# Flamingo block (gated cross-attention and gated feed-forward): scores, transposes and attention products of a query tile issued in one run each, turned probabilities kept in place

## What is computed

```python
# x: (16, 512, 512), context: (16, 120, 512)
Q, K, V = heads(layernorm(x) @ W_q.T), heads(ctx @ W_k.T), heads(ctx @ W_v.T)
scores = Q @ K^T / sqrt(32) - slope[head] * (query_pos - key_pos)       # 512 x 120 for each head
e = exp(scores - max(scores))
attn = e / (1.0 + sum(e))
x = x + tanh(g_xattn) * ((attn @ V) @ W_o.T)
n = layernorm(x);  prev = n shifted by one token
r = sigmoid((mu_r*n + (1-mu_r)*prev) @ W_r.T)
k = relu((mu_k*n + (1-mu_k)*prev) @ W_k.T) ** 2
x = x + tanh(g_ffn) * r * (k @ W_v.T)
```

## Time and profile before

| | |
|---|---|
| Time, median of 3 runs | 1523.38 us (1522.04 to 1524.48) |
| Span of the profiled execution, first to last instruction | 1519.6 us |
| TensorE matmul busy | 1442.7 us (95%) |
| TensorE weight loads busy | 1083.1 us (71%) |
| VectorE busy | 1161.5 us (76%) |
| ScalarE busy | 889.5 us (59%) |
| GpSimd busy | 721.3 us (47%) |

### The profile page before, as it was taken

The page is one execution under the profiler, slowest core; times in us unless marked ns, Lnnn a source line. Parts: engine busy times, 40 slices in busy tenths (PEclk is TensorE's granted clock), DMA queues, the critical chain, the costliest instruction groups (busy, mean ns, idle before and its releaser), DMA issues.

```text
span 1519.6 us, 32873 instructions
## 1 busy us (share of the span) xinstructions
PE 1442.7 (95%) x10864; PEld 1083.1 (71%) x10864; DVE 1161.5 (76%) x2889; ACT 889.5 (59%) x2928; POOL 721.3 (47%) x766
## 2 busy tenths in 40 slices
PE   7988899999999999999999999999999999999998
PEld 6876767677676767667686766767676676768667
DVE  4456868787887868798786879878687887868775
ACT  5147474665747465574747566473756657475662
POOL 0003455545455555545555464545546454555542
PEclk9999999999999999999999999999999999999999
DMA  8721001020200102020010202011020101001000
GB/s 270 215 66 49 8 29 50 0 76 0 56 20 28 49 0 76 0 56 20 28 49 14 62 0 56 20 36 41 14 62 0 56 20 53 23 27 50 1 30 28
DMA packets 53009, 65.95 MB, mean 43 GB/s; under 512 B 23024, under 2 KB 29168, under 8 KB 52976
## 3 DMA queue, kind: packets, MB, share of 16 engines
q1 hardware_dynamic: 52976, 65.52, 14.6%
HBM read 40.87 MB, written 24.64 MB: 43 GB/s over the span
## 4 chain that ended last, share of the span: by engine, by line
PE 48%; DVE 34%; issue 11%; ACT 3%; DMA 2%; DVEq 1%; SPq 0%; POOL 0%; ACTq 0%; POOLq 0%
PE rotating L401 33%; DVE probs L1038 7%; PE probs_bank L561 5%; DVE diff L1100 4%; PE score_bank L460 4%; DVE mix_k L1095 4%; PE attn_bank L575 3%; DVE relu L1100 3%; DVE square L1095 2%; PE score_bank L401 2%; ACT probs L773 2%; DVE mask_in L1137 2%; DVE stats L1008 2%; DVE norm L1017 2%; DVE xs L1064 2%
## 5 line engine op out<-in xcount | busy, mean ns | idle before, releaser
L773 ACT ACTIVATE probs<-probs,neg_max 128x120 f32<-128x120 f32 x1024 | 391.2, 385 | 29.6 <-DVE neg_max L1042 29.6
L1320 POOL TENSOR_TENSOR probs<-probs,recip 128x960 f32<-128x960 f32 x128 | 229.7, 1794 | 237.5 <-DVE recip L1053 237.5
L401 PE MATMUL rotating<-mixed_key,w_key 128*128 128x512 f32 x720 | 205.0, 413 | 24.8 <-ACT gated L825 24.8
L401 PE MATMUL rotating<-w_proj,attn_t 128*128 128x512 f32 x768 | 220.9, 417 | 2.9 <-DVE xnt_or_act L1023 2.0
L781 ACT COPY probs_t<-probs_bank 120x512 f32<-120x512 f32 x256 | 149.8, 585 | 121.3 <-PE probs_bank L561 121.1
L1038 DVE SCALAR_TENSOR_TENSOR probs<-mask_in,score_bank 128x120 f32<-128x120 f32 x1024 | 213.0, 269 | 9.5 <-PE score_bank L460 9.5
L401 PE MATMUL rotating<-w_value,xnt_or_act 128*128 128x512 f32 x720 | 202.3, 409 | 10.2 <-DVE xs L1064 10.2
L401 PE MATMUL rotating<-w_gate,mixed_gate 128*128 128x512 f32 x768 | 209.7, 409 | 0.0
L401 PE MATMUL rotating<-xnt_or_act,w_query 128*128 128x256 f32 x1536 | 198.7, 286 | 0.5 <-DVE xnt_or_act L1023 0.5
L773 ACT ACTIVATION_READ_ACCUMULATOR probs<-probs,neg_max 128x1 f32 x1024 | 194.0, 189 | 0.0
L401 PEld LDWEIGHTS rotating<-xnt_or_act,w_query 128*128 128x128 f32 x1536 | 187.7, 191 | 1.9 <-DVE xnt_or_act L1023 0.8
(11 more groups left out here) (126 smaller groups left out, 2167.7 us busy)
## 6 DMA issues: line engine op xcount, KB each, us to landing
xs<-in_x_dram SPq DMA_DIRECT2D x64, 256.0 KB, 2.9
out_dram<-gated SPq DMA_DIRECT2D x64, 256.0 KB, 3.0
value_scratch<-gated SPq DMA_DIRECT2D x16, 240.0 KB, 2.6
mask_in<-in_mask_dram SPq DMA_DIRECT2D x16, 240.0 KB, 2.6
keys_t<-key_scratch SPq DMA_DIRECT2D x16, 240.0 KB, 3.6
values<-value_scratch SPq DMA_DIRECT2D x16, 240.0 KB, 3.8
probs<-in_ctx_t_dram SPq DMA_DIRECT2D x6, 480.0 KB, 7.0
key_scratch<-query_t SPq DMA_DIRECT2D x12, 240.0 KB, 5.1
```

Source lines behind the costliest of these rows:

```text
L401: mm = pe.matmul(bank, stationary(a, c), moving(b, c), start=(i == 0), stop=(i == MATMULS - 1))
L773: e = act.activation(probs[:, t % 2, head, :], probs[:, t % 2, head, :], ACT.Exp, bias=neg_max[:, t % 2, head:head + 1], accum_out=sums[:, ...
L1320: pool.tensor_tensor(part, part, recip[:, t % 2, heads].unsqueeze(2).to_broadcast((P, H // 2, NK)), ALU.mult)\
```

## The change

The changed kernel computes the same thing with the same instructions on every engine; what changes is their order on TensorE, one buffer, and one wait on VectorE.

- `with_scores` becomes `all_scores`: all 16 products of a tile stand together, and the use that they were woven into follows whole.
- In `with_attention` the portions become 3, 3, 3, 3 (from 4, 3, 3, 2), and the four `attend` groups follow behind the last portion, where before `attend(g - 1)` stood behind `turn_probs(g)` and its portion.
- The scores of tile 2 stand right behind the attention of tile 0 and ahead of `key` 3; before they stood behind it.
- `probs_t` is no longer a buffer of its own with two slots by g. It lies over `probs` in one buffer `probs_room`, with a slot for each tile parity and each group. The transposed group is written over heads that have been transposed already; `probs` starts 128 elements later to make that safe.
- Since a slot of `probs` now holds what `attend` reads, `bias(b, t, 0)` waits for the attention of tile t - 2 (`attn_done`), where before it waited for that tile's transposes and exponentials.

```diff
-        probs = sb("probs", [P, 2, H, NK])
-        probs_t = sb("probs_t", [NK, 2, J, P])
+        HEAD_ROOM = G * J * (P - NK)
+        probs_room = sb("probs_room", [P, 2, HEAD_ROOM + H * NK])
+        probs = probs_room[:, :, HEAD_ROOM:].rearrange("p a (h k) -> p a h k", h=H)
+        probs_t = probs_room[0:NK].rearrange("k a (g j q) -> k a g j q", g=G, j=J)
...
-                                   values[:, head * HD:(head + 1) * HD], probs_t[:, g % 2, j, :],
+                                   values[:, head * HD:(head + 1) * HD], probs_t[:, t % 2, g, j, :],
...
-                def with_scores(t, what, tile, portions):
-                    at = 0
+                def all_scores(t):
                     for g in range(G):
                         scores(b, t, g)
-                        use(what, tile, range(at, at + portions[g]))
-                        at += portions[g]
-
-                def with_attention(t, what, tile, portions=(4, 3, 3, 2)):
+                def with_attention(t, what, tile, portions=(3, 3, 3, 3)):
                     at = 0
                     for g in range(G):
                         turn_probs(b, t, g)
                         use(what, tile, range(at, at + portions[g]))
                         at += portions[g]
-                        if g > 0:
-                            attend(b, t, g - 1)
-                    attend(b, t, G - 1)
-
-                with_scores(0, "gate", 0, (3, 3, 3, 3))
+                    for g in range(G):
+                        attend(b, t, g)
+                all_scores(0)
+                use("gate", 0)
                 use("gate", 1)
                 use("key", 0)
-                with_scores(1, "key", 1, (3, 3, 3, 3))
+                all_scores(1)
+                use("key", 1)
                 with_attention(0, "key", 2)
+                all_scores(2)
                 use("key", 3)
-                with_scores(2, "proj", 0, (3, 3, 3, 3))
+                use("proj", 0)
                 use("value", 0)
                 with_attention(1, "value", 1)
-                with_scores(3, "gate", 2, (4, 4, 4, 0))
+                all_scores(3)
+                use("gate", 2)
...
-                act.copy(probs_t[:, g % 2], probs_bank[0:NK, :].rearrange("k (j q) -> k j q", j=J))\
+                act.copy(probs_t[:, t % 2, g], probs_bank[0:NK, :].rearrange("k (j q) -> k j q", j=J))\
...
-                        dve.wait_ge(probs_turned, (b * QT + t - 1) * G)
-                        dve.wait_ge(exp_done, (b * QT + t - 1) * G)
+                        dve.wait_ge(attn_done, b * QT + t - 1)
```

More of the change, by code:

```diff
@@ L138, in flamingo_block @@
         wv_split = mixed_gate
-        ctx_raw = probs[:].rearrange("p a h k -> p (a h k)").rearrange("p (a c k) -> p a c k", a=4, k=CK)
+        ctx_raw = probs_room[:].rearrange("p a n -> p (a n)")[:, 0:2 * CT * CK]\
+            .rearrange("p (a c k) -> p a c k", a=2, k=CK)
         ctx_split = [xnt_or_act[:].rearrange("p s c t -> p (s c t)")[:, i * 2 * CT * CK:(i + 1) * 2 * CT * CK]
```

## The result

| | before | after |
|---|---|---|
| Time, median | 1523.38 us (1522.04 to 1526.69, 11 runs) | 1526.84 us (1525.75 to 1529.84, 11 runs) |
| Span of the profiled execution | 1519.6 us | 1523.9 us |

The account below looks back on a forecast made before the run. Bound: TensorE between 715.88 and 744.54 of a loop batch, VectorE before and ScalarE then VectorE after. 0.54 + 0.08 = 0.62 us a batch; 15 x 0.6 = 9, less 2 for batch 0: 1523.4 + 7 = 1530 us, range 1517 to 1536.

Parts of the forecast that it names:

- TensorE's savings become waits outside the middle stretch: Loop batch: TensorE savings, 4.0 us in TensorE time alone, can count only between 715.88 and 744.54, where TensorE shows no wait.
- Score run of 1.10 us: Scores of one tile in one run hold TensorE for 1.10 us, 1.3 to 1.4 us less TensorE time a tile.
- Attention run of 1.19 us: Four attention groups in a run hold TensorE for 1.19 us, a further group costing 0.28.
- Fourth transposes at the same place, held by ScalarE's list: Tile 0: fourth transposes start at 725.66 as before, waiting for a copy behind `act_split(1)`; about 1.3 us saved becomes waiting.
- Attention later, since it has been moved behind them: Tile 0: attention ends at 728.13 instead of 727.34, 0.8 us later, two attention groups having moved behind the fourth transposes.
- The chain `key` 3, relu 3, square 3, low part 3 delays `value` 0: After tile 0's attention, through ScalarE and GpSimd: `value` 0 starts at about 736.06, 0.54 us later than before.
- Nobody collects the early scores of tile 2: VectorE's list has tile 1's reciprocals ahead of tile 2's bias, so tile 2's scores ahead of `key` 3 go uncollected.
- The new wait on `attn_done` costs nothing: VectorE's bias: zero cost, as tile t - 2's attention already precedes tile t's scores on TensorE; without that cover, up to 1.19 us.
- Batch 0 gives 2 us: First batch, without relu chain or `act_split`: savings can count there, taken as 2 us of gain, between 0 and 4.0.
- The terms cancel: 1520.5 to 1526.5: No-change rival for the whole kernel: shift within -0.1 and +0.3 us a batch, 1520.5 to 1526.5 us, chance 0.25.
- Outside the middle stretch a saving just becomes a longer wait: Loop batch before 715.88 and after 744.54: a TensorE saving there only lengthens a wait and does not count.
- a sign of being wrong: Counted from tile 1's scores: prediction wrong if `value` 0 starts before +19.6, transposes' waits don't appear, or VectorE's chain changes length.

Follow-up runs that it names:

- e6: Changed kernel with the copy of tile 0's third group of transposed probabilities ahead of act_split(1) in ScalarE's list; 1516.52 us, ratio 0.9958.
- e3: Changed kernel with the attention groups woven between the transposes again (portions 4, 3, 3, 2); 1521.53 us, ratio 0.9984.
- e5: Changed kernel with only its attention part kept, scores woven as before the change and tile 2's behind key 3; 1532.63 us, ratio 1.0060.
- e1: Changed kernel with the scores of tile 2 moved back behind key 3, still in one run; 1519.74 us, ratio 0.9973.
- e4: Changed kernel with only its score runs kept: attention woven as before the change, scores of tile 2 behind key 3; 1512.86 us, ratio 0.9921.
- e9: e8 with the copy of tile 0's third group moved ahead of act_split(1) in ScalarE's list; 1501.35 us, ratio 0.9851.
- e10: e9 with the scores of tile 0 woven with gate 0 again; 1498.45 us, ratio 0.9839.
- e2: Changed kernel with the scores of tile 0 woven with gate 0 again, 3 steps behind each group; 1528.89 us, ratio 1.0029.
- e7: e6 with the scores of tile 0 woven with gate 0 as well; 1517.88 us, ratio 0.9959.
- e8: e4 with act_split(2) ahead of the exponentials of tile 1's first group in ScalarE's list; 1508.32 us, ratio 0.9901.

## Why the prediction was right, and where not

Slower by a little was right, in range and in sign: 1530 us forecast, 1526.8 measured. The forecast was +7 us as -2 + 9, the profile has -3.5 + 6.4 + 1.4. That start and tail together are -2.1, close to the -2 forecast, is in part luck: they hold two falls of the clock, 1.5 us before and 1.6 us after, which cancel.

- *TensorE's savings become waits outside the middle stretch.* Right: matmul busy time fell by 60 us and the time did not fall.
- *Score run of 1.10 us.* Right.
- *Attention run of 1.19 us.* Measured 1.01. A further group in the run costs (1.01 - 0.35) / 3 = 0.22, not the 0.28 that one row with two groups gave. That is 0.18 us less at each of the two tiles. Against it `value` 0 starts 0.15 us behind low part 3, not 0.06, and tile 1 takes 0.12 more than forecast otherwise (9.04 us for 9.10 with the shorter run). 0.62 - 0.18 + 0.09 - 0.18 + 0.12 = 0.47.
- *Fourth transposes at the same place, held by ScalarE's list.* Right to the hundredth when laid over VectorE's bias, and the waits stand in the full-clock batch: 0.86 us for GpSimd, 0.71 for ScalarE. e6 showed the cause by removing it.
- *Attention later, since it has been moved behind them.* Right. e3 and e5 show it from both sides: without it 5 us less, it alone 9 us more than before.
- *The chain `key` 3, relu 3, square 3, low part 3 delays `value` 0.* Right, 0.45 for 0.54 us. What I did not see is the second chain (split 2 behind the exponentials) close behind it, which left e1 at 7 instead of 17 us. The wait ahead of `value` 0 was 1.10 us, not 1.3, since the attention run is shorter.
- *Nobody collects the early scores of tile 2.* Not contradicted: e1 is faster with later scores.
- *The new wait on `attn_done` costs nothing.* Not tested alone: every run keeps it. e4 has it and is 11 us faster than before, so at most it costs little.
- *Batch 0 gives 2 us.* It gave 2.5. The 1.0 more in batch 1 is the 1.5 of `proj` 3's clock before, less the 0.4 that batch 1 loses like the others.
- *The terms cancel: 1520.5 to 1526.5.* The sum is off by 0.6: a shift of -0.1 to +0.3 gives 1519.9 to 1525.9. Nothing hangs on it.
- *Outside the middle stretch a saving just becomes a longer wait.* Wrong as stated. The wait ahead of `key` 0 grew from 1.66 to 2.88 us, and TensorE came out of it at 1.2 GHz. I took the scores of tile 1 to start when the bias ends; they start up to 1.5 us later. So in such a batch all my marks counted from that start are off: the fourth transposes came at +8.3, not +9.8, and `value` 0 at +18.6, not +20.2, though the places that they stood for were right. One of them was a sign of being wrong, `value` 0 earlier than +19.6, and the batch with the slow `key` 0 gives that sign; so does the absence of the transposes' waits in it. In the batch at full clock the marks hold: the fourth transposes at +9.78, the end of the attention of tile 0 at +12.1, `value` 0 at +20.1. In the loop of the changed kernel the loss ends in the waits ahead of the third and fourth transposes.
- *The tail.* Not in my sum. There `gate` 1 took 4.58 instead of 2.98 us behind an idle time that was the same before (2.81 and 2.82 us), and nothing hides it: 1.6 of the 4.3 us of the profiled execution. It is not the change's, since e5 and e9 have it too and e6 and e10 do not. Why the clock fell after one such wait and not after another stays open.

## What to carry to other kernels

An engine without a gap is not an engine that sets the pace: compute when each of its inputs is ready from the other engines' lists, and a saving counts only as far as the next of these times. Work that fits into such a wait is better woven into it than batched behind it, even where the batch itself is cheaper (here the attention groups); a batch pays where it shortens the way to the next result that someone waits for (here the scores). When a change is eaten up, look into the in-order list of the engine that is waited for: here two entries moved there and the half of the change that paid turned +3.5 us into -22 (e9), and -25 with the scores of tile 0 woven again (e10). And what a lower clock costs depends on the waits behind it: it was free in the changed kernel and had a price in the faster ones.

## What the runs showed of the hardware that was not expected

TensorE's clock: behind an idle time of 2.8 to 2.9 us the granted clock was at 1.2 GHz for a part of the next 12 steps in 11 of the changed kernel's 15 `key` 0 (4.3 to 5.5 us instead of 3.0), behind 1.55 to 1.69 us in none of those of the kernel before, e2, e5, e7 or e10. The length of the last wait alone does not decide it: behind the 2.00 us ahead of `proj` 3 in batch 0 it fell in six of twelve executions, and behind the 2.81 to 2.84 us in the tail in nine of twelve. The cost stayed hidden as long as waits for other engines followed (88.3 us a batch with and without), and came out at 0.6 us in a batch of e3, e4, e6 and e8 and at 1.0 us in one of e9, where the waits behind it had been shortened. The Trainium skill (TensorE: Matmul & The Clock Gate, What's actually happening) tells of the same two levels; the traces agree with that.

A further group of four attention products cost less in a run of four groups (0.22 us) than in a run of two (0.28 us).
